# Last attention layer: heads 0-7 on partitions 0-63, heads 8-15 on partitions 64-127, and a head's second scores alternate with first scores of the other half

## The reference

```python
def _mha(x, wi, bi, wo, bo):
    B, S, D = x.shape
    hd = D // NHEAD                    # 16 heads of 8 features
    q, k, v = jnp.split(x @ wi.T + bi, 3, axis=-1)
    q, k, v = (heads(q), heads(k), heads(v))
    scores = jnp.einsum('bhqd,bhkd->bhqk', q, k) / jnp.sqrt(jnp.asarray(hd, x.dtype))
    attn = jax.nn.softmax(scores, axis=-1)
    o = jnp.einsum('bhqk,bhkd->bqhd', attn, v).reshape(B, S, D)
    return o @ wo.T + bo
```

## Time and profile before

| | |
|---|---|
| median of 3 executions | 3424.13 us (3422.94 to 3424.37) |
| profiled execution | 3428.36 us, its span 3426.5 us |
| mean granted clock of TensorE | 0.865 of full speed |
| busy in the span | PE 75%, PEld 55%, DVE 65%, ACT 48%, POOL 23% |
| the attention changed | first scores at 2590 us, last exponential at 3040 us |

### The profile page before, as it was taken

The page is one execution under the profiler, slowest core; times in us unless marked ns, Lnnn a source line. Parts: engine busy times, 40 slices in busy tenths (PEclk is TensorE's granted clock), DMA queues, the critical chain, the costliest instruction groups (busy, mean ns, idle before and its releaser), DMA issues. The chain is left out here.

```text
span 3426.5 us, 72224 instructions
## 1 busy us (share of the span) xinstructions
PE 2583.1 (75%) x20196; PEld 1895.2 (55%) x20196; DVE 2229.6 (65%) x4923; ACT 1637.5 (48%) x3655; POOL 783.2 (23%) x1119
## 2 busy tenths in 40 slices
PE   2657759999897575999359999966567999972380
PEld 1334533469787432999237777756344666651270
DVE  5967874248787522677766666545976888864267
ACT  2545413334364232677536666632254777751253
POOL 0001100000000165555432222200151222203553
PEclk7899869999998688999689999958787999975685
DMA  3092000100091011222594556400086655610123
GB/s 98 0 256 93 31 0 28 32 14 0 10 152 56 21 44 43 68 71 67 172 230 60 69 74 72 51 1 0 0 260 67 75 69 74 74 33 23 55 78 104
DMA packets 305861, 233.52 MB, mean 68 GB/s; under 512 B 26012, under 2 KB 287564, under 8 KB 305420
## 3 DMA queue, kind: packets, MB, share of 16 engines
q1 hardware_dynamic: 277976, 195.57, 29.4%
q0 software_dynamic: 19072, 28.28, 2.9%
q10 hardware_dynamic: 8704, 8.39, 0.8%
HBM read 132.49 MB, written 96.51 MB: 67 GB/s over the span
## 5 line engine op out<-in xcount | busy, mean ns | idle before, releaser
L2534 ACT ACTIVATE h_pt<-h_ps 128x384 f32<-128x384 f32 (+1 forms) x1024 | 543.0, 544 | 279.5 <-PE h_ps L2443 143.8
L2283 DVE TENSOR_REDUCE h_nm<-h_ps 128x4 f32<-128x1024 f32 (+1 forms) x448 | 539.9, 1219 | 158.2 <-PE h_ps L2414 62.2
L1623 POOL DMA_INDIRECT sorted_rows<-e_row,e_pos x192 | 184.6, 962 | 435.3 <-DVE e_row L1602 239.8
L1813 POOL DMA_INDIRECT results<-e_y,e_ykey x208 | 210.9, 1014 | 194.8 <-DVE e_y L1802 177.2
L2462 PE MATMUL h_ps_o<-h_pt,h_vp 128*32 128x256 f32 (+1 forms) x4096 | 246.8, 358 | 1.3 <-ACT h_pt L2534 1.3
L1860 ACT ACTIVATE e_hid<-e_ps_h,e_wt 128x128 f32<-128x128 f32 x688 | 203.7, 369 | 27.3 <-PE e_ps_h L1834 17.7
L1842 PE MATMUL e_ps_o<-e_wt,e_hid 128*128 128x128 f32 x1376 | 199.5, 284 | 10.3 <-ACT e_hid L1860 6.9
L1770 DVE TENSOR_SCALAR e_wt<-w 128x1156 f32 (+1 forms) x208 | 139.7, 672 | 102.6 <-DVE e_y L1802 71.2
L1834 PE MATMUL e_ps_h<-e_hT,e_wt 128*128 128x128 f32 x1376 | 201.2, 287 | 4.6 <-issue 2.1
L2448 PE MATMUL h_ps<-h_sq,h_sk 128*128 128x256 bf16 x1024 | 193.9, 275 | 9.8 <-ACT h_pt L2534 5.7
L2385 PE MATMUL h_ps<-h_sk,h_sq 128*128 128x256 bf16 x1024 | 160.4, 281 | 39.4 <-DVE h_identb L2265 37.1
(11 more groups left out here) (448 smaller groups left out, 6424.5 us busy)
## 6 DMA issues: line engine op xcount, KB each, us to landing
h_sk<-k_stack SPq DMA_DIRECT2D x192, 128.0 KB
q_stack<-p_parts SPq DMA_DIRECT2D x64, 256.0 KB, 3.3
h_sq<-q_stack SPq DMA_DIRECT2D x64, 256.0 KB
sorted_rows<-pad SPq DMA_DIRECT2D x26, 520.0 KB, 10.8
e_xt<-sorted_rows SPq DMA_DIRECT2D x104, 130.0 KB
e_got<-results SPq DMA_DIRECT2D x24, 512.0 KB, 4.4
k_stack<-p_parts SPq DMA_DIRECT2D x32, 384.0 KB, 3.1
v_ones<-p_v SPq DMA_DIRECT2D x32, 288.0 KB, 3.3
```

What stands on the lines that cost most here:

```text
L1623: gp.indirect_dma_start(xs[:, :], bass.IndirectOffsetOnAxis(ap=pos[:, n % choices, tile:tile + 1], axis=0), row[n % ROWS][:, :], None).the ...
L1813: gp.indirect_dma_start(ys[:, :], bass.IndirectOffsetOnAxis(ap=key[m // 4][:, m % 4:m % 4 + 1], axis=0), y[m][:, :], None).then_inc(return ...
L2283: dve.tensor_reduce(to, got, AX, ALU.max, negate=True).then_inc(s["mx"].sem, 1)
L2534: act.activation(pt[g % 2][:, j, :], ps_2[:, h % 2, 0:SW], ACT.Exp, scale=scale).then_inc(s["ex"].sem, 1)
```

## The change

Heads 0 to 7 lie on partitions 0 to 50 and heads 8 to 15 on partitions 64 to 114, eight heads beside each other. `load_halves` fills both halves with six DMAs each (they were six in all). Score matmuls use the 64 partitions of their head's half. `both_scores` replaces `scores` and `pair_scores` in this layer: for head h it issues, alternating, two second-score matmuls of entry b and two first-score matmuls of entry b+2 for a head of the other half. So each unit of first scores is written in two pieces, one at each of two heads. Units come in the order of heads 8 to 15, then 0 to 7. The maxima are kept in the order of the halves and moved with two DMAs instead of three. Four DMAs of ones are added at the beginning of `project("p3")`. The causal attention before it keeps its order and tiling.

```diff
-HEAD_LOADS = 6
+HEAD_LOADS = dict(h2=6, h3=12)
...
+                        else:
+                            for u in range(SLOTS):
+                                sp.dma_start(buffers["sk"][u][64 + KR:64 + KM, 0:NH // 2, :], ones_rows[:, 0:NH // 2, :]
+                                             ).then_inc(ones_in, 16)
...
+                h0 = (2 * k + HH) % NH
+                to, got = nm[n][:, h0:h0 + 2, :], pair.rearrange("p o (q c) -> p o q c", q=TPB)
...
+                                    for f in range(HALVES):
+                                        gp.dma_start(sq[nxt[0]][64 * f + KR:64 * f + KM, 0:HH, :],
+                                                     mT[3 * HH * f:3 * HH * (f + 1), :]).then_inc(maxima_in[tag], 16)
...
+                        def both_scores(b, u, later, h, first, body):
+
+                            if body:
+                                if h == 0:
+                                    maxima_moved(pe, b)
+                                pe.wait_ge(*at("ex", b, h - 1))
+                                f, i = divmod(head(h), HH)
+                                rows = slice(64 * f, 64 * (f + 1))
+                            if first:
+                                n, un, rn = b + 2, later[0], later[1]
+                                if h % 2 == 0:
+                                    unit_free(n, un, rn, h // 2)
+                                fm, im = divmod((h + HH) % NH, HH)
+                                rows_m = slice(64 * fm, 64 * (fm + 1))
+                            for t in range(TPB):
+                                if body:
+                                    ins = pe.matmul(ps_2[:, h % 2, t * SEQ:(t + 1) * SEQ], sk[u][rows, i, t * P:(t + 1) * P],
+                                                    sq[u][rows, i, :], start=True, stop=True)
+                                    if t == TPB - 1:
+                                        ins.then_inc(s["s2"].sem, 1)
+                                if first:
+                                    ins = pe.matmul(ps_1[:, h % 4, t * SEQ:(t + 1) * SEQ], sq[un][rows_m, im, t * P:(t + 1) * P],
+                                                    sk[un][rows_m, im, :], start=True, stop=True)
+                                    if t == TPB - 1 and h % 2 == 1:
+                                        ins.then_inc(s["s1"].sem, 1)
...
+        def load_halves(sp, b, u, up):
+
+            cols = ds(b * SEQ, SEQ)
+            hh, two = NH // 2, 2 * HD
+            q_rows, k_rows = (d.rearrange("a (e h) t -> (a e) h t", h=NH)[:, :, cols] for d in (q_parts, k_parts))
+            slot_q, slot_k = heads_in["sq"][u], heads_in["sk"][u]
+            for f in (1, 0):
+                lo, heads = 64 * f, slice(hh * f, hh * (f + 1))
+                sp.dma_start(slot_q[lo:lo + 2 * two, 0:hh, :], q_rows[0:2 * two, heads, :]).then_inc(up, 16)
+                for n, part in ((0, 1), (1, 1), (2, 0)):
+                    sp.dma_start(slot_k[lo + n * two:lo + (n + 1) * two, 0:hh, :], k_rows[part * HD:part * HD + two, heads, :]
+                                 ).then_inc(up, 16)
+                sp.dma_start(slot_q[lo + 2 * two:lo + KR, 0:hh, :], q_rows[3 * HD:5 * HD, heads, :]).then_inc(up, 16)
+                sp.dma_start(slot_q[lo + KR:lo + KM, 0:hh, :], heads_in["sk"][0][KM:2 * KM - KR, 0:hh, :]).then_inc(up, 16)
```

More of the change, by code:

```diff
@@ L325, in build @@
                 ("otc", 1), ("out", 1), ("x", 1))},
-            loaded=[SlotSignal(pool, f"{t}_loaded{u}", 16 * (HEAD_LOADS + 1), u + 4, 4) for u in range(4)]) for t, units in (("h2", 6), ("h3", 8))}
+            loaded=[SlotSignal(pool, f"{t}_loaded{u}", 16 * (HEAD_LOADS[t] + 1), u + 4, 4) for u in range(4)]) for t, units in (("h2", 6), ("h3", 8))}
         z_s, z_n, z_g, z_a = sig("z_shifted", 1), sig("z_normed", 1), sig("z_gain", 1), sig("z_done", 1)
@@ L2232, in maxima_moved @@
                 def maxima_moved(eng, b):
-                    eng.wait_ge(maxima_in[tag], b * 48 + 48)
+                    eng.wait_ge(maxima_in[tag], (b + 1) * 16 * (3 if causal else 2))
                 def ahead(u, r, n):
@@ L2376, in unit_free @@
                             elif k == 0:
-                                pe.wait_ge(*s["loaded"][u].last(r, 16 * (HEAD_LOADS + 1)))
+                                pe.wait_ge(*s["loaded"][u].last(r, 16 * (HEAD_LOADS[tag] + 1)))
                             pe.wait_ge(*at("mx", b, k - 1))
[L2380 to L2387, removed]
+                        def both_scores(b, u, later, h, first, body):
[22 more added lines that the diff above has]
+                                        ins.then_inc(s["s1"].sem, 1)
@@ L2419, in max_scores @@
                         def max_scores(b, u, r, h):
[L2421 to L2424, removed]
                             half, i = h // 8, h % 8
@@ L2438, in scores @@
                             o, hd = ps_2[:, h % 2, :], head(h)
[L2439 to L2449, removed]
+                            pe.matmul(o[:, 0:SEQ], sk[u][:, hd, 0:P], sq[u][:, hd, :], start=True, stop=False, skip_group_check=True)
+                            pe.matmul(o[:, SEQ:SW], sk[u][:, hd, P:2 * P], sq[u][:, hd, P:], start=False, stop=False,
+                                      skip_group_check=True)
+                            ins = pe.matmul(o.rearrange("p (t q) -> p t q", q=SEQ)[:, :, 0:P], mskb[:, 0:P],
+                                            mskb[:, 2 * P:3 * P].unsqueeze(1).to_broadcast([P, 2, P]),
+                                            start=False, stop=True, skip_group_check=True)
                             ins.then_inc(s["s2"].sem, 1)
@@ L2477, in turn_max @@
                                 ins = pe.matmul(ps_m[0:3 * NH, q * P:(q + 1) * P],
-                                                mpart[:, q, :, :].rearrange("p a h -> p (a h)"), identb[:, :], start=True, stop=True)
+                                                mpart[:, q, :, :, :].rearrange("p f a h -> p (f a h)"), identb[:, :], start=True, stop=True)
                             ins.then_inc(s["mt"].sem, 1)
@@ L2497, in step @@
                                 g, j = h // HG, h % HG
-                                if body:
+                                if not causal:
+                                    both_scores(b, u, later, h, first, body)
+                                elif body:
                                     scores(b, u, h)
@@ L2521, in step @@
                                     project_out(b - 1)
-                                if first:
+                                if first and causal:
                                     max_scores(b + 2, *later, h)
```

41 lines of the change are left out of this document (21 added, 20 removed).

## The result

The changed kernel takes 3434.52 us in the median of six executions (3432.13 to 3437.77), the kernel before 3423.02 (3422.03 to 3424.37). The ratio is 1.0033, with a 95% interval of 1.0021 to 1.0046: slower, by 11.5 us, where +24 was forecast. The sign held, by the circuit through VectorE. The larger term of the forecast, loads that land late ((14.2 - 13.71) x 28 = 13.7 of the 24 us), did not come, so what happened is rival 1 (3433), in its size and in its mechanism.

The account below looks back on a forecast made before the run. TensorE was taken as the bound (346 of 350 us busy). 28 steps with a load 18.5, two steps 0.3, start 4: +23 us, rounded with the last steps' shape changes to +24, median 3448; range 3412 to 3510.

Parts of the forecast that it names:

- the circuit through VectorE: Last attention layer: weighing inside a two-head score unit makes TensorE wait for VectorE's maximum; 13.71 us a step against 13.54.
- loads that land late: Last layer's loads of a batch entry land at B + 13.1, 1 us late, making a step 14.2 us; chance 0.46.
- rival 1: Last layer: loads arrive in time and waits rule, 13.7 us a step, 3433 us (3425 to 3440); chance 0.18.
- The overlap and its price: Last layer's scores: both array halves stream at once, four matmuls in 0.22 us; each change of shape costs 0.10 us.
- group 3: Third group of four heads in a step: 3.15 us, through ScalarE's copy of the sums and exponentials.
- The dear end: Upper cost of SyncE's load issues, 0.65 us for one of k_stack; last issue 9.2 us after the first.
- the cheap end: Lower cost of SyncE's load issues, 0.376 us each; last issue 7.2 us after the first.
- Time to landing: From the last load's issue to its data's arrival: 3.3 us, taken from SyncE's nearest issue.
- B: Start of the third head in a group of four heads, from which the prediction counts times in us.
- The start: Before the attention begins: 24 more load issues, taken as +4 us, from 0 to +8.5.
- rival 4: Faster: half-height scores leave the array without drain, 12.9 us a step, 3409; if all waits gave way, 3358; chance 0.14.

Follow-up runs that it names:

- experiment 1: The changed kernel with a head's second scores alternating with first scores of the same half, so the four matmuls can't overlap; 3486.61 us.
- Experiments 1 to 4: Changed kernel with, in turn: halves not overlapping, 3486.61 us; maxima over half the keys, 3421.96; first-score units in one piece, 3418.61; weighing one head earlier, 3406.69.
- experiment 6: The changed kernel with its loads split once more, into 24 DMAs of four heads each, and the values; 3617.26 us.
- experiment 7: The changed kernel with each weighing cut in two pieces, after the second and fourth head of a group; 3385.81 us.
- experiment 5: The kernel before, with its last layer's loads split by heads into 12 DMAs of half the size; 3426.27 us, ratio 1.0008.

## Why the prediction was right about the waits and wrong about the loads

- *The overlap and its price* (four matmuls in 0.22 us, 0.10 us per change of shape): right. The pair's rows and experiment 1 show it.
- *The circuit TensorE - VectorE - TensorE, 13.71 us a step* (group 3 through ScalarE): right, 13.77, group by group. Its terms as written add up to 3.02 and 3.16 where it has 3.03 and 3.15, which changes nothing. Experiments 1 to 4 take it apart: longer width lengthens it (15.22 against 15.1), a shorter maximum shortens it until ScalarE's takes over, and moving the weighing out of the unit opens it. The shape of the result, less work and more time, is shown by that.
- *The loads, 14.2 us a step*: wrong, and this is the step that failed. It was two mis-sized terms of one sum. The twelve issues were put at 8.2 us from the first to the values; they took 6.5 (2802.44 to 2808.94). The dear end, 0.65 us for one load of k, was a misreading: a merged row (1.95 for three) holds the gaps between its issues too. One such issue took 0.56 us before and takes 0.37 now (ns min/median/max; the kernel before, then the changed one):

```profile
L2574 SPq DMA_DIRECT2D h_sk<-k_stack x78: 563/564/592, 2652.2 to 2992.6; - x78
```
```profile
L2610 SPq DMA_DIRECT2D h_sk<-k_stack x155: 316/374/798, 2651.3 to 2999.5; - x155
```

  Even the cheap end, 7.2, was above the 6.5. Time to landing was put at 3.3 us, from a store's row; experiment 6 has 2.33 and experiment 7 2.45, and the changed kernel, which never waits for a load, doesn't show its own. So loads are in at B + 1.6 + 6.5 + 2.3 = B + 10.4, 1.7 us before the B + 12.1 at which they are needed. The issues alone decide it: with 3.3 us to landing it would still be B + 11.4. The mechanism itself is shown by experiment 6, in which the step grows by 5.7 us, and it returns in experiment 7 at a step of 12.03; in the change it stays hidden, as rival 1 said.
- *The start, +4 us*: about half. From the first transposition of the projection to the first scores it was 2487.9 to 2590.4 us before and is 2483.0 to 2587.8: 2.3 us more. The 24 added issues cost little because none was held up now. Three loads of k in the last slot, before and then in the changed kernel:

```profile
2578.80 5.26 SPq L2574 DMA_DIRECT2D h_sk<-k_stack  x3
```
```profile
2578.30 1.49 SPq L2610 DMA_DIRECT2D h_sk<-k_stack  x3
```

  That it was full queues that held them up before, as the prediction has it, no view here shows; the issues took about 1.7 us each instead of 0.56.
- *The rest of the sum.* 30 steps by 0.22 are 6.6 us, the start 2.3. About 2.6 of the 11.5 us remain. In the profiled executions the stretch from the projection's first transposition to the start of the last exponential grew from 552.5 to 563.2 us, 10.7, so nearly all of the loss is in the changed stages. By the turnings of the maxima the first two steps took 24.0 us instead of 22.3, and the last two 27.4 instead of 26.6; the steady 0.22 a step explains 0.4 of each difference. In the first ones the clock is lower (0.71 from 2600 to 2625 us, 0.81 before):

```profile
2600.00:2625.00 25.00, 21.05 (x184) 8.12 (x182) 20.14 (x19) 14.10 (x27) 6.35 (x18) 0.71 0.04 10
```
```profile
2600.00:2625.00 25.00, 23.55 (x186) 13.16 (x187) 21.65 (x21) 13.53 (x25) 8.21 (x24) 0.81 0.01 3
```

The first row is the changed kernel's, the second that of the kernel before.

- *What it would have taken.* The chances gave the loads 0.46 with one 1-us lateness worked out from two estimates, each wide by more than that 1 us; the waits alone, worked out from the rows, had 0.18. When a rival stands on measured terms and the forecast adds one on estimates, the former deserved more.
- *Faster (rival 4)*: the changes of shape kept their price; nothing left the array sooner. Its last sum is written wrong: 3424 - 70 is 3354, and 3358 holds the +4 of the start.

## What to carry to other kernels

Where two engines hand a two-deep buffer back and forth, look at what the producer does between the two halves of one buffer: a long block there is paid in the circuit, even if both engines have idle time. Halving the time of the bound engine's score matmuls gained nothing until that block was moved to a boundary between buffers (0.4% faster) and then cut in two (1.2%). Neither move was tried in the kernel before, which waited up to 0.87 us a step, so part of the first gain may not need the halves. With each circuit opened the next one was near: VectorE's, ScalarE's, then the loads'. Count a circuit from rows, group by group, before counting on a share of busy time; and cost the issue of a smaller DMA from single issues of the nearest form, not from a merged row.

## What the runs showed of the hardware

The time of a DMA packet depended on the DMA's form. The kernel before, then the changed one, in the DMA view from 2650 to 3000 us:

```profile
q1 hardware_dynamic: 49241, 24.93, 58.4%
```
```profile
q1 hardware_dynamic: 50487, 24.45, 25.8%
```

Share x 16 engines x 350 us by the packets gives 66 ns a packet before and 29 ns after, and 30 ns in experiment 5, which has the old partitions. SyncE's issue of a load of k fell as well, from 0.56 to 0.37 us, and GpSimd's moves of the maxima land sooner:

```profile
h_sq<-h_mT POOLq DMA_DIRECT2D x52, 12.0 KB, 2.8
```

It was 5.7 us; in experiment 5, with the three moves of before, it is 3.3. Why a load of 16 heads has slower packets than two of 8 wasn't tried; it can be the number of packets waiting at a time or the form itself. The Trainium skill (DMA: Bandwidth & Descriptors, Rules for kernel authors) advises one transfer instead of two on disjoint partition halves; here the two cost SyncE time and relieved the DMA engines, and in the changed kernel neither mattered for the time. The Trainium skill (TensorEngine Tiling (Array Packing), Key Properties) says that changing the tiling mode drains the array. The 0.10 us at each change of shape agrees, also out of the half-height form: the weighing at 2804.80 starts 0.32 us after the pair at 2804.48, as it did before.
